# One-core transformer stack on Trainium2: router and adapter biases added by VectorE, the relative attention's output bias issued ahead of its products, and linear attention's score matmuls in alternating halves

## The chip, the cores and the metric

The kernel runs on one core of one Trainium2 chip. The metric is the device time of one launch in microseconds (us): the median over several runs. Two versions of one program are compared.

## The reference

Eight layers are applied, one after the other, to x of shape (8, 512, 128) in float32: x = x + layer(layernorm(x)). Cut to the four layers that the change touches:

```python
# ffn (twice): mixture of 8 experts, each token weighs its best 2
logits = xt @ Ws + bs
topk_w, topk_idx = top_k(logits, 2); topk_w = softmax(topk_w)
combine = sum(one_hot(topk_idx, 8) * topk_w[..., None], axis=1)
y = (silu(xt @ Wg[e]) * (xt @ Wu[e])) @ Wd[e]           # per expert e
out = einsum('ted,te->td', y, combine)
# linear attention: 16 heads of 64
weights = (queries @ keys^T / 8) * decay                  # masked scores
out = (weights @ values + beta * values) @ Wout
# adapter (twice): weights top_w of 2 adapters from the mean over all tokens
h = gelu(x @ down_w^T + down_b) * top_w
out = h @ up_w^T + (top_w[:, :, None] * up_b).sum(axis=1)[:, None, :]
# relative attention: 16 heads of 8, softmax with relative positions
out = attention(...) @ Wp.T + bp
```

The other layers are two softmax attentions without biases.

## The kernel before

One batch element of 512 tokens is one turn, and a hardware loop makes eight turns. x stays in on-chip memory through all eight layers of a turn. Tokens are cut into NT = 4 tiles of 128. Every engine runs its own program, written out by hand in the order of the layers (`pe_norm`, `pe_attn`, `pe_norm`, `pe_moe`, and so on for TensorE, with `act_...`, `pool_...` and VectorE's functions beside them). They meet at semaphores alone, so nothing but the order of the code and these waits sets what runs when.

Between two layers stands the norm. VectorE adds the layer's result to x in two halves of two tiles (`add_to_x`, L1312), takes mean and variance, GpSimd computes the inverse deviation (L437), VectorE writes the rows (L1303), TensorE transposes them (L790), and ScalarE copies them to xnT (L596). The next layer's first matmul waits for xnT.

Places that the change and the prediction touch:

- Router (`pe_moe`, L964 and L965). For each token tile one matmul of xnT with Ws (8 columns) and one of a row of ones with the bias row, both into bank 6. After the fourth pair `m_logit` lets VectorE start its chain over the logits (from L1397 on), and TensorE starts the experts' gate and up products (L984 and L988, 512 columns). VectorE's first product for the experts (L1441) is queued behind the chain over the logits. The third up product waits for it.
- Linear attention (`pe_lin`). For each of eight pairs of heads c, `scores(c)` makes two times four matmuls (L1047), head 2c on partitions 0 to 63 into bank 0, head 2c+1 on partitions 64 to 127 into bank 1. VectorE masks each bank (L1496). `states(c)` (L1059) follows, ScalarE copies its result (L695), VectorE sums it (L1504, L1505), and `outputs(c)` (L1074, L1078), one iteration later, waits for that sum. From c = 3 on `transposes(c-3)` (L1087) closes the iteration, and ScalarE copies it (L685) ahead of the next copy of states.
- Adapter (`pe_adapter`). Four down products (L1109), a small gate product, a transpose of the mixing weights (L1115, ScalarE copies it in L712), then per token tile four up matmuls (L1122) and one matmul of the mixing weights with `up_b` (L1123), 8 rows deep, into the same bank. The first up matmul waits for L712's copy, for the gelus (L710) and for VectorE's scaled up weights (L1559).
- Output projection of the attentions (`pe_out`). Four transposes (L839), ScalarE's copy (L761 in relative attention), then per tile one matmul (L844), in relative attention followed by one of a row of ones with the bias row (L846), which lies on partition 96.

A float32 matmul of this kernel stands in the trace as two records with a weight load (PEld) each; a transpose is one record.

Of the kernel before, what the change touches and what calls it, by code (L numbers as in the profile page):

```python
# [74 lines left out]
def build(nc, a_x, a_wq, a_wk, a_wv, a_wo, b_wattn, b_wout, m_ws, m_bs, m_wg, m_wu, m_wd,  # L75
# [10 lines left out]
    with ExitStack() as ctx:  # L86
# [3 lines left out]
        def sem(name):  # L90
            return ctx.enter_context(nc.semaphore(name))
# [29 lines left out]
        bs_row = wd[96:97, 2, NF - 1, 0:E]  # L121
# [119 lines left out]
        def bank(n):  # L241
# [117 lines left out]
        d_wTs = sem("ad_mix_column")  # L359
        d_y = sem("ad_up_products")  # L360
# [14 lines left out]
            (ws[:, :], m_ws), (bs_row, m_bs.rearrange("(a n) -> a n", a=1)),  # L375
# [328 lines left out]
        def act_adapter(eng, n):  # L704
# [7 lines left out]
            eng.activation(d_wT[0:E, :], bank(5)[0:E, 0:P], ACT.Copy).then_inc(d_wTs, 1)  # L712
# [123 lines left out]
        def pe_out(eng, n, w_out, bias):  # L836
# [3 lines left out]
            m.then_inc(a_oT, 1)  # L840
            eng.wait_ge(a_oTs, n + 1)
            for t in range(NT):
                o = bank(1 + t // 2)[:, P * (t % 2):P * (t % 2) + P]
                m = eng.matmul(o, xnT[:, P * t:P * t + P], w_out, start=True, stop=bias is None)  # L844
                if bias is not None:
                    m = eng.matmul(o, ones_row, bias, start=False, stop=True)  # L846
                if t % 2 == 1:
                    m.then_inc(a_y, 1)
# [111 lines left out]
        def pe_moe(eng, n):  # L960
            eng.wait_ge(experts_in, 16 * len(expert_loads))
            eng.wait_ge(xnT_ok, 2 * n + 2)
            for t in range(NT):
                eng.matmul(bank(6)[:, E * t:E * t + E], xnT[:, P * t:P * t + P], ws[:, :], start=True, stop=False)  # L964
                m = eng.matmul(bank(6)[:, E * t:E * t + E], ones_row, bs_row, start=False, stop=True)  # L965
# [28 lines left out]
        def pe_lin(eng):  # L994
# [44 lines left out]
            def scores(c):  # L1039
                for r in range(2):  # L1040
                    h = 2 * c + r
                    if h >= 2:
                        eng.wait_ge(l_wts, h - 1)
                    else:
                        eng.wait_ge(l_qk, 2 * NC2)
                    for t in range(NT):
                        m = eng.matmul(bank(r)[:, P * t:P * t + P], l_kT[64 * r:64 * r + 64, c, P * t:P * t + P],  # L1047
                                       l_qT[64 * r:64 * r + 64, c, P * t:P * t + P], start=True, stop=True)
                    m.then_inc(l_sc, 1)
# [56 lines left out]
        def pe_adapter(eng, n):  # L1106
# [8 lines left out]
            eng.transpose(bank(5)[0:E, 0:P], d_w[:, :], ident[:, :]).then_inc(d_wTp, 1)  # L1115
            eng.wait_ge(d_wTs, n + 1)
            eng.wait_ge(d_hs, KD * (n + 1))
            eng.wait_ge(d_ups, n + 1)
            for t in range(NT):
                o = bank(4 + t // 2)[:, P * (t % 2):P * (t % 2) + P]  # L1120
                for k in range(KD):
                    eng.matmul(o, d_hid[:, k, P * t:P * t + P], d_up[:, k, :], start=(k == 0), stop=False)  # L1122
                m = eng.matmul(o, d_wT[0:E, :], up_b[:, :], start=False, stop=True)  # L1123
                if t % 2 == 1:
                    m.then_inc(d_y, 1)

# [582 lines left out]
```

## Time and profile before

| | |
|---|---|
| median of 3 runs | 4981.29 us (4979.67 to 5001.24) |
| profiled execution | 4969.21 us, its span 4967.5 us |
| busy: TensorE, VectorE, ScalarE, GpSimd | 90%, 48%, 35%, 17% of the span |
| mean granted TensorE clock | 0.912 of full speed |
| chain that ended last | TensorE 80% |
| DMA over the span | 17.25 MB, 3 GB/s |

The share of busy time counts matmuls by modelled ends; the clock is one of two levels, 1.0 (2.4 GHz) or 0.5 (1.2 GHz), and 0.912 is its mean. Times below are microseconds from the start of the span, in the profiled execution.

### The profile page before, as it was taken

How to read it: one execution, taken by the hardware profiler on the slowest of the kernel's cores; microseconds unless marked ns; L12 is line 12 of the kernel's file. 1: busy time of each engine (PE TensorE's matmuls, PEld its weight loads, DVE VectorE, ACT ScalarE, POOL GpSimd, SP SyncE). 2: the span in 40 equal slices, each digit the busy share in tenths (PEclk: the TensorE clock that was granted, in tenths of full speed). 3: DMA queues.
4: the chain of work that ended last, by engine and by line, in shares of the span. 5: the costliest groups of instructions: out<-in, count | busy, mean ns of one | idle time of the engine just before them, and what ended most of it. 6: DMA issues, size and time to landing. Idle time of an engine off the chain costs nothing.

```text
span 4967.5 us, 76834 instructions
## 1 busy us (share of the span) xinstructions
PE 4473.0 (90%) x30219; PEld 2776.4 (56%) x30275; DVE 2379.6 (48%) x6906; ACT 1719.1 (35%) x3496; POOL 843.7 (17%) x1441
## 2 busy tenths in 40 slices
PE   7998989889898898988989889899898998989989
PEld 3556645565455654556545575455754457545575
DVE  3435634356443554435544355444554445544455
ACT  2322432325333343333433234333343333433334
POOL 2003110031100311103011040111401114011130
PEclk8989979999899998999989999899998999998989
DMA  2000000000000000000000000000000000000000
GB/s 68 1 1 1 1 6 1 1 1 1 6 1 1 1 1 6 1 1 1 1 6 1 1 1 1 6 1 1 2 1 6 1 1 2 1 3 1 1 1 3
DMA packets 19571, 17.25 MB, mean 3 GB/s; under 512 B 2462, under 2 KB 18799, under 8 KB 19183
## 3 DMA queue, kind: packets, MB, share of 16 engines
q1 hardware_dynamic: 19183, 11.99, 0.8%
q8 instruction: 254, 4.16, 0.4%
q14 instruction: 134, 1.10, 0.1%
HBM read 9.89 MB, written 2.10 MB: 2 GB/s over the span
## 4 chain that ended last, share of the span: by engine, by line
PE 80%; DVE 6%; POOL 6%; ACT 5%; issue 3%; DVEq 0%; ACTq 0%; POOLq 0%; SPq 0%
PE banks L984 7%; PE banks L974 7%; PE banks L988 7%; PE banks L880 7%; PE banks L908 6%; PE banks L825 6%; PE banks L920 3%; POOL work L478 3%; PE banks L865 3%; PE banks L1180 3%; PE banks L1201 2%; PE banks L1167 2%; PE banks L1074 2%; PE banks L1047 2%; PE banks L1023 2%
## 5 line engine op out<-in xcount | busy, mean ns | idle before, releaser
L1369 DVE CUSTOM_DVE_ANT_0 work<-banks,mask_row 128x512 f32<-128x512 f32 (+3 forms) x1024 | 451.6, 488 | 274.0 <-PE banks L880 270.6
L880 PE MATMUL banks<-work 32*128 32x512 f32 (+3 forms) x2048 | 526.7, 493 | 11.4 <-DVE work L1369 11.4
L908 PE MATMUL banks<-work 32*128 32x256 f32 (+3 forms) x2048 | 512.7, 504 | 20.8 <-ACT work L638 20.8
L638 ACT ACTIVATE work<-banks 128x384 f32<-128x384 f32 (+1 forms) x768 | 368.9, 526 | 441.9 <-PE banks L908 440.3
L437 POOL TENSOR_TENSOR rstd<-rstd,half 128x2 f32<-128x2 f32 x128 | 87.5, 703 | 2451.2 <-DVE moments L1297 1834.2
L654 ACT ACTIVATE work<-banks 128x512 f32<-128x512 f32 (+1 forms) x384 | 228.8, 596 | 687.6 <-PE banks L984 687.4
L1441 DVE TENSOR_TENSOR work<-work,banks 128x512 f32<-128x512 f32 (+1 forms) x384 | 263.5, 686 | 344.8 <-PE banks L988 344.5
L984 PE MATMUL banks<-xnT,wg 128*128 128x512 f32 (+1 forms) x768 | 417.8, 627 | 0.0
L988 PE MATMUL banks<-xnT,wu 128*128 128x512 f32 (+1 forms) x768 | 406.1, 611 | 0.0
L447 POOL TENSOR_SCALAR_AFFINE_SELECT work<-work 128x128 f32<-128x128 f32 (+1 forms) x768 | 252.6, 332 | 897.4 <-ACT work L638 886.1
L974 PEld LDWEIGHTS banks<-wd,work 128*128 128x128 f32 (+1 forms) x3072 | 360.6, 191 | 57.3 <-issue 57.3
L880 PEld LDWEIGHTS banks<-work 32*128 32x128 f32 x2048 | 259.0, 198 | 216.8 <-DVE work L1369 141.3
L974 PE MATMUL banks<-wd,work 128*128 128x128 f32 (+1 forms) x3072 | 361.0, 274 | 0.0
L1599 DVE TENSOR_TENSOR work<-work,banks 128x512 f32<-128x512 f32 (+1 forms) x384 | 229.2, 599 | 269.6 <-PE banks L1169 238.1
L908 PEld LDWEIGHTS banks<-work 32*128 32x128 f32 x2048 | 252.3, 198 | 125.3 <-ACT work L638 80.0
L825 PE MATMUL banks<-work,values 128*9 128x512 f32 (+3 forms) x1024 | 290.7, 433 | 0.0
L790 PE MATMUL banks<-ident,xn 128*128 128x128 f32 x256 | 85.3, 418 | 215.2 <-DVE xn L1303 212.4
L749 ACT ACTIVATE work<-banks 128x512 f32<-128x512 f32 x256 | 139.1, 595 | 377.3 <-PE banks L1201 377.3
L1426 DVE SCALAR_TENSOR_TENSOR x<-banks,work,x 128x128 f32<-128x128 f32 x512 | 144.2, 344 | 248.3 <-PE banks L974 248.3
L988 PEld LDWEIGHTS banks<-xnT,wu 128*128 128x128 f32 (+1 forms) x768 | 143.8, 187 | 206.1 <-issue 206.1
L740 ACT ACTIVATE work<-banks,work 128x512 f32<-128x512 f32 (+3 forms) x512 | 229.5, 543 | 43.4 <-DVE work L1604 43.4
L1604 DVE TENSOR_REDUCE work<-banks 128x1 f32<-128x512 f32 (+3 forms) x512 | 216.4, 483 | 22.9 <-PE banks L1180 22.9
(255 smaller groups left out, 7254.4 us busy)
## 6 DMA issues: line engine op xcount, KB each, us to landing
x_next<-in_L_attn_a_x_dram SPq DMA_DIRECT2D x8, 256.0 KB, 2.8
out_dram<-x SPq DMA_DIRECT2D x8, 256.0 KB, 2.2
wg<-in_L_ffn_Wg_dram SPq DMA_DIRECT2D x1, 1376.0 KB
wu<-in_L_ffn_Wu_dram SPq DMA_DIRECT2D x1, 1376.0 KB
wd<-in_L_ffn_Wd_dram SPq DMA_DIRECT2D x2, 512.0 KB
wk_l<-in_L_attn_a_Wk_dram SPq DMA_DIRECT2D x1, 512.0 KB, 7.8
wv_l<-in_L_attn_a_Wv_dram SPq DMA_DIRECT2D x1, 512.0 KB, 6.5
wq_l<-in_L_attn_a_Wq_dram SPq DMA_DIRECT2D x1, 512.0 KB, 7.2
```

Of the source, the lines that this page charges most:

```text
L447: eng.affine_select(out=v, in_=v, compare_op=ALU.is_ge, fill=0.0, base=0, pattern=[[0, 2], [1, P]] if j == 2 else [[1, P]], channel_multip ...
L638: eng.activation(prob4[:, G % 2, hh, C_AT[j]:C_AT[j] + C_N[j]], bank(3 + c % 3)[:, 0:C_N[j]], ACT.Exp).then_inc(s_exp, 1)
L740: eng.activation(r_prob[:, h % 2, at[t]:at[t] + (t + 1) * P], bank(bk)[:, col:col + (t + 1) * P], ACT.Exp, bias=r_neg_max[:, h % 2, t:t + ...
L825: m = eng.matmul(bank(bk)[row:row + HD + 1, P * s:T], values[:, s, h, :], p_cols[:, h % 2, at:at + T - P * s], start=(s == 0), stop=(s == ...
L880: m = eng.matmul(bank(k % 3)[:, col:col + N], q4[own, G, P * t:P * t + P], k4[own, G, 0:N], start=True, stop=True)
L908: m = eng.matmul(bank(3 + c % 3)[:, col:col + N], k4[own, G, P * s:P * s + P], q4[own, G, P * s:T], start=True, stop=True)
L974: m = eng.matmul(bank(4 + e % 2)[:, P * t:P * t + P], hidden[0:w, e % 2, j, P * t:P * t + P], wd[0:w, e, j, :], start=(j == 0), stop=(j == ...
L984: eng.matmul(bank(i % 2)[0:w, :], wg[:, e, f0:f0 + w], xnT[:, :], start=True, stop=True).then_inc(m_g, 1)
L988: eng.matmul(bank(2 + i % 2)[0:w, :], wu[:, e, f0:f0 + w], xnT[:, :], start=True, stop=True).then_inc(m_u, 1)
L1369: m = eng.tensor_tensor_reduce(out=summed[:, k % 2, col:col + N], in0=bank(k % 3)[:, col:col + N], in1=mask_row[:, T - N:T], scale=1.0, sc ...
L1441: eng.tensor_tensor(hidden[0:w, e % 2, j, :], silu[0:w, i % 2, :], bank(2 + i % 2)[0:w, :], ALU.mult).then_inc(m_h, 1)
L1599: eng.tensor_tensor(v, v, bank(k % 2)[:, 0:JOB_N[j]], ALU.add).then_inc(r_sum, 1)
```

## The change

Four things are edited.

1. Router: the four bias matmuls go. The bias is loaded once, spread over all partitions (`bs_all`), and VectorE's copy of the logits becomes an addition of it.
2. Adapter: of the four bias matmuls one stays, issued after the first tile's up matmuls, into bank 7. VectorE adds that bank to all four tiles of x in one operation ahead of `add_to_x`, which waits for it. The transposed mixing weights go to bank 6, and TensorE waits for ScalarE's copy of them only ahead of the bias matmul.
3. Relative attention's projection: the four bias matmuls are issued ahead of the wait for ScalarE's copy, and the products add to them.
4. Linear attention: `scores(c)` loops over tiles outside and halves inside, with one wait for both halves' earlier masks at its start.

```diff
@@ loads
-        bs_row = wd[96:97, 2, NF - 1, 0:E]
+        bs_all = sb("bs_all", [P, E])
-            (ws[:, :], m_ws), (bs_row, m_bs.rearrange("(a n) -> a n", a=1)),
+            (ws[:, :], m_ws), (bs_all[:, :], bass.AP(m_bs.tensor, m_bs.offset, [[0, P], [1, E]])),
@@ act_adapter
-            eng.activation(d_wT[0:E, :], bank(5)[0:E, 0:P], ACT.Copy).then_inc(d_wTs, 1)
+            eng.activation(d_wT[0:E, :], bank(6)[0:E, 0:P], ACT.Copy).then_inc(d_wTs, 1)
@@ pe_out
             m.then_inc(a_oT, 1)
+            out = [bank(1 + t // 2)[:, P * (t % 2):P * (t % 2) + P] for t in range(NT)]
+            if bias is not None:
+                for t in range(NT):
+                    eng.matmul(out[t], ones_row, bias, start=(t % 2 == 0), stop=False, skip_group_check=True)
             eng.wait_ge(a_oTs, n + 1)
             for t in range(NT):
-                o = bank(1 + t // 2)[:, P * (t % 2):P * (t % 2) + P]
-                m = eng.matmul(o, xnT[:, P * t:P * t + P], w_out, start=True, stop=bias is None)
-                if bias is not None:
-                    m = eng.matmul(o, ones_row, bias, start=False, stop=True)
+                m = eng.matmul(out[t], xnT[:, P * t:P * t + P], w_out, start=bias is None, stop=True,
+                               skip_group_check=True)
@@ pe_moe
-                eng.matmul(bank(6)[:, E * t:E * t + E], xnT[:, P * t:P * t + P], ws[:, :], start=True, stop=False)
-                m = eng.matmul(bank(6)[:, E * t:E * t + E], ones_row, bs_row, start=False, stop=True)
+                m = eng.matmul(bank(6)[:, E * t:E * t + E], xnT[:, P * t:P * t + P], ws[:, :], start=True, stop=True)
@@ pe_lin, scores(c)
-                for r in range(2):
-                    h = 2 * c + r
-                    if h >= 2:
-                        eng.wait_ge(l_wts, h - 1)
-                    else:
-                        eng.wait_ge(l_qk, 2 * NC2)
-                    for t in range(NT):
+                if c >= 1:
+                    eng.wait_ge(l_wts, 2 * c)
+                else:
+                    eng.wait_ge(l_qk, 2 * NC2)
+                for t in range(NT):
+                    for r in range(2):
                         m = eng.matmul(bank(r)[:, P * t:P * t + P], l_kT[64 * r:64 * r + 64, c, P * t:P * t + P],
                                        l_qT[64 * r:64 * r + 64, c, P * t:P * t + P], start=True, stop=True)
-                    m.then_inc(l_sc, 1)
+                        if t == NT - 1:
+                            m.then_inc(l_sc, 1)
@@ pe_adapter
-            eng.transpose(bank(5)[0:E, 0:P], d_w[:, :], ident[:, :]).then_inc(d_wTp, 1)
-            eng.wait_ge(d_wTs, n + 1)
+            eng.transpose(bank(6)[0:E, 0:P], d_w[:, :], ident[:, :]).then_inc(d_wTp, 1)
             eng.wait_ge(d_hs, KD * (n + 1))
             eng.wait_ge(d_ups, n + 1)
             for t in range(NT):
                 o = bank(4 + t // 2)[:, P * (t % 2):P * (t % 2) + P]
                 for k in range(KD):
-                    eng.matmul(o, d_hid[:, k, P * t:P * t + P], d_up[:, k, :], start=(k == 0), stop=False)
-                m = eng.matmul(o, d_wT[0:E, :], up_b[:, :], start=False, stop=True)
+                    m = eng.matmul(o, d_hid[:, k, P * t:P * t + P], d_up[:, k, :], start=(k == 0), stop=(k == KD - 1))
                 if t % 2 == 1:
                     m.then_inc(d_y, 1)
+                if t == 0:
+                    eng.wait_ge(d_wTs, n + 1)
+                    eng.matmul(bank(7)[:, 0:P], d_wT[0:E, :], up_b[:, :], start=True, stop=True).then_inc(d_bias, 1)
@@ VectorE, moe
-                link(eng.tensor_copy(lg[:, :, :], bank(6)[:, 0:NT * E].rearrange("p (t e) -> p t e", t=NT)))
+                link(eng.tensor_tensor(lg[:, :, :], bank(6)[:, 0:NT * E].rearrange("p (t e) -> p t e", t=NT),
+                                       bs_all[:, :].unsqueeze(1).to_broadcast([P, NT, E]), ALU.add))
@@ VectorE, adapter
                 i.then_inc(d_ups, 1)
+                eng.wait_ge(d_bias, n + 1)
+                eng.tensor_tensor(x[:, :, :], x[:, :, :], bank(7)[:, 0:P].unsqueeze(1).to_broadcast([P, NT, P]),
+                                  ALU.add).then_inc(d_based, 1)
+                eng.wait_ge(d_based, n + 1)
                 return add_to_x(4, d_y, n)
```

TensorE's instructions at the adapter, a row for each run of equal ones (output, operands, shape, how many). Before:

```order
L1109 MATMUL banks<-xnT,downT 128x512 x3
L1115 MATMUL banks<-ident,work 8x128
L1122 MATMUL banks<-work 128x128 x4
L1123 MATMUL banks<-up_b,work 128x128
L1122 MATMUL banks<-work 128x128 x4
L1123 MATMUL banks<-up_b,work 128x128
L1122 MATMUL banks<-work 128x128 x4
L1123 MATMUL banks<-up_b,work 128x128
L1122 MATMUL banks<-work 128x128 x4
L1123 MATMUL banks<-up_b,work 128x128
L790 MATMUL banks<-ident,xn 128x128 x4
```

In the changed kernel (L1124 are the up matmuls, L1129 is the bias, with what they wait for):

```order
L1118 MATMUL banks<-ident,work 8x128 [waits ad_mix]
L1124 MATMUL banks<-work 128x128 [waits ad_up_scaled,ad_hidden]
L1124 MATMUL banks<-work 128x128 x3
L1129 MATMUL banks<-up_b,work 128x128 [waits ad_mix_column]
L1124 MATMUL banks<-work 128x128 x12
```

Three bias matmuls have gone, and the wait for the mixing column has moved behind the first four up matmuls.

TensorE's instructions at the end of relative attention, before (w_r is the output weight, wd the tile in which the ones and the bias row lie):

```order
L839 MATMUL banks<-ident,xn 128x128 x4
L844 MATMUL banks<-w_r,xnT 128x128
L846 MATMUL banks<-wd 128x128
L844 MATMUL banks<-w_r,xnT 128x128
L846 MATMUL banks<-wd 128x128
L844 MATMUL banks<-w_r,xnT 128x128
L846 MATMUL banks<-wd 128x128
L844 MATMUL banks<-w_r,xnT 128x128
L846 MATMUL banks<-wd 128x128
```

And in the changed kernel:

```order
L841 MATMUL banks<-ident,xn 128x128 x4
L846 MATMUL banks<-wd 128x128 x4
L849 MATMUL banks<-w_r,xnT 128x128 x4
```

The four bias matmuls stand together behind the transposes, and the four products stand together behind them.

VectorE's instructions at the end of the adapter in the changed kernel (L1567 is the new addition, L1316 `add_to_x`):

```order
L1564 TENSOR_SCALAR work<-upT,work 128x128 x3
L1567 TENSOR_TENSOR x<-x,banks 128x512 [waits ad_mixed_bias]
L1316 TENSOR_TENSOR x<-x,banks 128x256 [waits ad_up_products,ad_bias_added]
L1299 BN_STATS stats<-x 128x6 [waits layer_done]
L1299 BN_STATS stats<-x 128x6
```

One operation over all of x has come in between the scaling of the up weights and the first half's addition.

## Rows read from the trace of the kernel before

**Rows 1.** The page, part 4: the chain that ended last, by engine.

```profile
PE 80%; DVE 6%; POOL 6%; ACT 5%; issue 3%; DVEq 0%; ACTq 0%; POOLq 0%; SPq 0%
```

**Rows 2.** Groups of instructions by line: records | busy us, mean ns | idle before.

```profile
L965 PE MATMUL banks<-wd 1*128 1x8 f32 x128 | 37.9, 367 | 0.0
L1123 PE MATMUL banks<-up_b,work 8*128 8x128 f32 x128 | 30.9, 321 | 0.0
```

**Rows 3.** Timeline of TensorE at a router: start, length, engine, line, records.

```profile
899.34 0.57 PE L964 MATMUL banks<-ws,xnT 128*128 128x8 f32 x2 [0.56 <-ACT xnT L596]
899.84 0.59 PE L965 MATMUL banks<-wd 1*128 1x8 f32 x2
...
903.50 1.22 PE L984 MATMUL banks<-xnT,wg 128*128 128x512 f32 x1
```

**Rows 4.** Timeline of TensorE at linear attention's beta logits.

```profile
974.52 1.86 PE L998 MATMUL banks<-wbeta,xnT 128*128 128x16 f32 x8 [0.56 <-ACT xnT L596]
976.22 1.20 PE L1023 MATMUL banks<-xnT,wq_l 128*128 128x512 f32 x1
```

**Rows 5.** Windows: busy per engine; behind POOL's the granted clock, DMA share, GB/s.

```profile
899.30:903.50 4.20, 4.16 (x16) 4.00 (x17) 0.00 (x0) 0.00 (x0) 0.00 (x0) 0.50 0.02 4
903.50:908.50 5.00, 5.00 (x7) 2.18 (x7) 4.04 (x13) 2.11 (x3) 0.00 (x0) 0.50 0.00 0
974.50:976.20 1.70, 1.68 (x8) 1.70 (x9) 0.00 (x0) 1.18 (x1) 0.67 (x1) 0.50 0.00 0
976.20:980.20 4.00, 4.00 (x8) 1.75 (x8) 0.75 (x2) 1.63 (x4) 0.00 (x0) 0.50 0.00 0
```

**Rows 6.** Timeline behind another router (first L984 at 748.64).

```profile
752.36 0.68 DVE L1441 TENSOR_TENSOR work<-work,banks 128x512 f32<-128x512 f32 x1
...
754.03 0.16 PEld L988 LDWEIGHTS banks<-xnT,wu 128*88 128x88 f32 x1 [0.27 <-issue]
```

**Rows 7.** Timeline of an adapter, up matmuls and bias matmuls.

```profile
641.15 0.25 ACT L712 ACTIVATE work<-banks 8x128 f32<-8x128 f32 x1
641.45 1.16 PE L1122 MATMUL banks<-work 128*128 128x128 f32 x8 [0.82 <-ACT work L712]
...
642.95 1.16 PE L1122 MATMUL banks<-work 128*128 128x128 f32 x8
...
647.04 0.48 PE L1123 MATMUL banks<-up_b,work 8*128 8x128 f32 x2
```

**Rows 8.** Timeline at the end of relative attention.

```profile
1861.33 0.66 PE L839 MATMUL banks<-ident,xn 128*128 128x128 f32 x4 [0.68 <-DVE xn L1348]
...
1862.67 0.49 PE L844 MATMUL banks<-w_r,xnT 128*128 128x128 f32 x2 [0.69 <-ACT xnT L761]
...
1866.50 0.79 PE L846 MATMUL banks<-wd 1*128 1x128 f32 x2
```

**Rows 9.** Timeline of linear attention's output products.

```profile
1067.45 7.41 PE L1101 MATMUL banks<-wout_l,work 128*128 128x128 f32 x64 [0.69 <-ACT work L685]
```

**Rows 10.** Timeline: the scores of c = 2.

```profile
1025.38 1.71 PE L1047 MATMUL banks<-work 64*128 64x128 f32 x16
```

**Rows 11.** Windows, L1047 alone: matmuls (x) and weight loads (x) in flight in 0.01 us.

```profile
1025.86:1025.87 0.01, 0.01 (x3) 0.01 (x2) 1.00 0.00 0
1026.20:1026.21 0.01, 0.01 (x4) 0.01 (x4) 1.00 0.00 0
```

**Rows 12.** Timeline: linear attention's first masks, sum and outputs.

```profile
1019.13 1.29 DVE L1496 TENSOR_TENSOR work<-banks,keep_ge 128x512 f32<-128x512 f32 x2 [0.49 <-PE banks L1047]
...
1022.42 0.29 DVE L1505 TENSOR_TENSOR work<-work 128x128 f32<-128x128 f32 x1
...
1022.78 0.52 PEld L1074 LDWEIGHTS banks<-work 128*128 128x128 f32 x4
```

**Rows 13.** Timeline: linear attention's last two iterations.

```profile
1051.80 0.60 ACT L685 ACTIVATE work<-banks 128x512 f32<-128x512 f32 x1 [4.21 <-PE banks L1087]
...
1054.00 0.53 PEld L1074 LDWEIGHTS banks<-work 128*128 128x128 f32 x4
...
1057.15 0.60 ACT L685 ACTIVATE work<-banks 128x512 f32<-128x512 f32 x1 [4.21 <-PE banks L1087]
...
1059.02 0.93 PEld L1074 LDWEIGHTS banks<-work 128*128 128x128 f32 x4 [2.14 <-issue]
```

More of the change, by code:

```diff
@@ L359, in build @@
         d_wTs = sem("ad_mix_column")
+        d_bias = sem("ad_mixed_bias")
+        d_based = sem("ad_bias_added")
         d_y = sem("ad_up_products")
```

## The prediction

> **What bounds the kernel now.** I read the page's chain first: TensorE holds 80% of it, so time taken from TensorE's own stream counts unless a wait appears in its place [rows 1]. The groups by line give the size of the bias matmuls: 128 records of 37.9 us at the routers and 128 of 30.9 us at the adapters, none with idle time ahead of it [rows 2]. Busy time does not say what a removal is worth, so each place was read in the timeline: router, adapter, projection, scores. The windows give the clock that was granted there.
>
> **Router (edit 1).** A router's stretch runs from 899.34 to the first gate product at 903.50: 4.16 us for 16 records, one per 0.26 us [rows 3]. The nearest thing without bias matmuls is linear attention's beta product: four matmuls of the same weights' size, 8 records, 974.52 to the next product at 976.22, 1.70 us [rows 4]. Both run at the slow clock, 0.50 [rows 5]. So a router loses 4.16 - 1.70 = 2.46 us, and two routers in each of eight turns lose 16 x 2.46 = 39 us. The lower bound is that the products behind give half of it back through the clock (rival A), the upper one that they give none and the clock rises earlier. VectorE's addition in place of a copy is an operation on 32 columns; even at the price of a 512-column one, 0.68 us, it is covered: the chain over the logits ends in front of the L1441 at 752.36, that product is done at 753.04, and the weight load that waits for it starts only at 754.03, 1.0 us later [rows 6]. Were that cover gone, it would cost up to 0.68 us a router, 11 us. The broadcast load of 32 bytes per partition is issued once, at the start, and I count it as nothing.
>
> **Adapter (edit 2).** One record of this shape follows the other every (7.41 - 0.27) / 63 = 0.113 us where nothing interrupts them [rows 9]. A tile with its bias takes 642.95 - 641.45 = 1.50 us, of which eight up records need 8 x 0.113 = 0.90; the bias costs 0.60, far above its two records, since TensorE pauses ahead of it and behind it [rows 7]. Before, the stretch is 641.45 to 647.52, 6.07 us. After, the first tile with its bias takes 1.50, the second starts anew with 1.16 for eight records, and two more take 16 x 0.113 = 1.81: 4.47 us, a gain of 1.60. The start moves too: it waited for L712's copy, which began at 641.15 [rows 7], and now waits for the gelu that ends shortly behind that. The bounds are 0 and 0.30, I take 0.15. Together 1.75 us, 16 times: 28 us. VectorE's new operation covers 512 columns from a bank, as L1441 does in 0.68 us [rows 6]. The bias is ready some 1.5 us into the stretch, so it ends near 2.3 us, and the second tile's matmuls, for which `add_to_x` waits, end near 2.7 us. It is hidden behind them, with 0.4 us to spare; without that cover it would still be hidden ahead of the second half, because VectorE's first half and statistics have 1.8 us of matmuls over them. What is queued behind it on VectorE is the first half's addition alone.
>
> **Relative projection (edit 3).** In the typical turn products and biases run from 1862.67 to 1867.29, 4.62 us; TensorE had been free since 1861.99 [rows 8]. A matmul's two records last 0.79 us there when the clock has fallen, 0.49 before. After, the four biases start near 1862.0 and take what eight records of that size take, 1.16 us less the end of the last, and one pause of 0.2: the products start near 1863.0, 0.35 us later than before. They then run on for 1.16 us [as rows 7], to 1864.2. That is 3.1 us less. If the clock is fast throughout before too, each change between product and bias costs half of the adapter's (0.60 - 2 x 0.113), 0.19 us [rows 7, 9], a step of two records 0.42 us, eight of them 3.4 us, and the gain is 1.9; if it is slow throughout, everything about doubles and the gain is 2.4. I take 2.7 us, eight times: 22 us, between 15 and 25.
>
> **Scores in alternating halves (edit 4).** Sixteen records in sequence would need 16 x 0.113 + 0.16 = 1.97 us [rows 9]. They take 1.71 [rows 10], and in the middle of the stretch four matmuls and four weight loads are in flight where there were three and two before [rows 11]: the second half already runs beside the end of the first. If the halves run beside each other all the way, they take what eight records take, 1.16 us, 0.55 less. Not all of it arrives. In c = 0 and 1 VectorE sets the pace: both masks end at 1020.42 and the next scores need both; the outputs start at 1022.78, right behind the sum that ends at 1022.71 [rows 12]. Neither moves. From c = 4 on a chain takes over: transposes, ScalarE's copies L685 and L695, VectorE's sum, then the outputs. In the last iteration, where no scores cover it, it takes 1059.02 - 1057.15 = 1.87 us; one iteration earlier the outputs start 1054.00 - 1051.80 = 2.20 us behind the same copy [rows 13]. So 0.33 of the 0.55 us is worth something there. A turn gains 2 x 0.55 (c = 2, 3) + 4 x 0.33 = 2.4 us, eight turns 19 us. The bounds are 0 (the hardware orders them no better) and 8 x 8 x 0.55 = 35 us.
>
> **Sum.** 39 + 28 + 22 + 19 = 108 us. The profiled execution took 4969.2 us, which gives 4861; the median of the runs lies 12 us above that execution, and I put it back on: 4873 us.
>
> **Rivals.**
>
> A. The clock takes back half of the router's gain. The matmuls with 8 columns run at the slow clock, and so do the first products behind them, 4 to 5 us of them [rows 5]. If the clock rises at a set distance from the start of the router, 2.46 us of 512-column products move into the slow stretch and cost twice their time: 16 x 1.23 = 20 us less gain, 4893 us. Against it: the products are slow for 5.0 us behind a start of 4.16 us and for 4.0 us behind one of 1.70 us, so the rise follows the wide products more than the first matmul [rows 3 to 5].
>
> The Trainium skill, "TensorE: Matmul & The Clock Gate", Part 1, says that the warm-up is a budget of time and not a number of matmuls, and that whatever is issued in it runs at half speed. By that rule rival A's 4893 us would be the result. The trace leaves it open, since the slow stretch behind a short start is not longer by what the start is shorter.
>
> B. Alternation gives nothing, because VectorE's masks or the copies hold the loop. For it: one chain already stands within 0.33 us of deciding [rows 13]. Then 4892 us.
>
> C. The adapter's new addition comes late and holds the norm. That needs the 0.4 us of slack gone; it costs at most 0.68 us, 16 times: 4884 us.
>
> D, slower. Every change of half costs TensorE what the adapter's bias costs in its place, 0.60 us per matmul of two records [rows 7]. Eight matmuls take 4.8 us instead of 1.71, 3.1 us more for each of 64 pairs of heads, 198 us; with the other edits' 89 us gained the kernel comes out at 5090. The point from which it decides is (1.71 + 89/64) / 8 = 0.39 us for a matmul. Against it: halves do overlap where they meet [rows 11], and the bias shares its rows of the array with the matmuls around it, which the halves do not.
>
> **How the numbers follow.** The forecast, all four edits near their sizes, gets 0.66; A 0.13, B 0.12, C 0.04, D 0.05. The range goes down to 4845 (the alternation's upper bound and a clock that falls less often, as TensorE's stretches of small matmuls get shorter) and up to 4908, which holds A, B and C, and most of A with B (4912). What a measurement can tell from no change is about 0.5%, 25 us. All cases but D are faster than that, save a remainder.
>
> **What would show it.** Router: first router record to first gate product 1.7 us, where it was 4.16. Adapter: first up matmul to the last 4.5 us, with VectorE's new operation over before the second tile's matmuls. Projection: first product later by 0.3 us, last one ending 1.2 us behind it. Scores: 16 records in 1.2 us, periods of 5.0 us where they were 5.35 in the later iterations, and new idle time of TensorE ahead of L1074's counterpart. A: the slow stretches behind the routers longer by 2 us. D: scores above 3 us. The forecast is wrong if the clock is granted less in the experts' products, if an iteration of linear attention stays at 5.35 us, or if another stage, which no edit touches, waits more.

## The result, and the profile after

The changed kernel takes 4823.22 us, median of 4 runs (4816.55 to 4831.63), beside 4980.48 us for the kernel before on the same chip. The ratio is 0.9681, 95% interval 0.9645 to 0.9716: 157 us faster. The forecast was 4873 us, its range 4845 to 4908, so the kernel ends 50 us below the forecast and 22 us below the range. Medians take every run; ratios leave out runs that lie over 1.5% above the fastest of the same program. The profiled execution took 4821.89 us, span 4820.2 us, mean granted clock 0.929; before it was 4969.21, 4967.5 and 0.912.

The page of the changed kernel: busy time, the clock in 40 slices, and the chain that ended last.

```profile
PE 4323.8 (90%) x30051; PEld 2656.8 (55%) x30051; DVE 2385.6 (49%) x6922; ACT 1718.7 (36%) x3496; POOL 841.7 (17%) x1441
...
PEclk8999999999899999999989999999998999999989
...
PE 79%; DVE 7%; POOL 7%; ACT 4%; issue 3%; DVEq 0%; POOLq 0%; ACTq 0%; SPq 0%
```

The page of the kernel before, the clock line.

```profile
PEclk8989979999899998999989999899998999998989
```

The chain is what it was, to within a percentage point in each engine [rows 1]. The clock line is not: a 7 is gone and there are fewer 8s. Both programs are now read at the four places of the forecast.

**Router.** The changed kernel's timeline, TensorE and the addition of the bias.

```profile
866.62 1.85 PE L968 MATMUL banks<-ws,xnT 128*128 128x8 f32 x8 [0.56 <-ACT xnT L598]
868.32 1.20 PE L987 MATMUL banks<-xnT,wg 128*128 128x512 f32 x1
...
868.50 0.19 DVE L1401 TENSOR_TENSOR work<-banks,bs_all 128x32 f32<-128x32 f32 x1 [2.98 <-PE banks L968]
```

From the first record to the first gate product it is 1.70 us, where it was 4.16 [rows 3], to the hundredth what was forecast. The addition in place of the copy is 0.19 us long.

**Adapter.** The changed kernel's timeline.

```profile
624.04 0.69 ACT L712 ACTIVATE work<-banks,down_b 128x512 f32<-128x512 f32 x1 [0.17 <-PE banks L1112]
624.63 0.25 ACT L714 ACTIVATE work<-banks 8x128 f32<-8x128 f32 x1
...
624.78 1.16 PE L1124 MATMUL banks<-work 128*128 128x128 f32 x8 [0.67 <-ACT work L712]
...
625.87 0.48 PE L1129 MATMUL banks<-up_b,work 8*128 8x128 f32 x2
...
626.29 2.95 PE L1124 MATMUL banks<-work 128*128 128x128 f32 x24
626.39 0.69 DVE L1567 TENSOR_TENSOR x<-x,banks 128x512 f32<-128x512 f32 x1 [2.70 <-PE banks L1129]
627.55 0.42 DVE L1316 TENSOR_TENSOR x<-x,banks 128x256 f32<-128x256 f32 x1 [0.47 <-PE banks L1124]
```

The up products now wait for the gelu (L712) and start 0.15 us behind the start of the copy of the mixing column (L714), where it was 0.30 [rows 7]. They end at 629.24, 4.46 us behind their start (forecast 4.47, before 6.07). VectorE's new operation ends at 627.08, and the addition behind it begins 0.47 us later, released by TensorE and not by it.

**Relative attention's projection.** The changed kernel's timeline.

```profile
1807.88 0.65 PE L841 MATMUL banks<-ident,xn 128*128 128x128 f32 x4 [0.68 <-DVE xn L1352]
...
1808.46 1.15 PE L846 MATMUL banks<-wd 1*128 1x128 f32 x8
1808.57 0.60 ACT L763 ACTIVATE xnT<-banks 128x512 f32<-128x512 f32 x1 [2.08 <-PE banks L841]
...
1809.54 1.16 PE L849 MATMUL banks<-w_r,xnT 128*128 128x128 f32 x8
```

From the first transpose to the end of the products it is 1810.70 - 1807.88 = 2.82 us, before 1867.29 - 1861.33 = 5.96 [rows 8]. The biases fill the time of ScalarE's copy, and eight product records stand in one row of 1.16 us. All eight turns show this at the fast clock.

**Scores in alternating halves.** The changed kernel's timeline in two late iterations of linear attention.

```profile
1606.89 1.16 PE L1049 MATMUL banks<-work 64*128 64x128 f32 x16
1606.99 0.60 ACT L687 ACTIVATE work<-banks 128x512 f32<-128x512 f32 x1 [3.88 <-PE banks L1090]
...
1608.49 0.29 DVE L1510 TENSOR_TENSOR work<-work 128x128 f32<-128x128 f32 x1
...
1608.86 0.52 PEld L1077 LDWEIGHTS banks<-work 128*128 128x128 f32 x4
...
1611.90 1.16 PE L1049 MATMUL banks<-work 64*128 64x128 f32 x16
```

Sixteen records take what eight take, 1.16 us, where they took 1.71 [rows 10]. The period is 1611.90 - 1606.89 = 5.01 us, before 5.35. The outputs start right behind VectorE's sum (1608.86 beside 1608.78), so the chain from the copy to the sum does decide there, as read from [rows 13].

So all four places came out as forecast, and the kernel is still 50 us faster than forecast.

**Where the rest is.** I cut each turn into its stages, from the first transpose of one norm (L790, in the changed kernel L792) to that of the next. Means over the eight turns of the profiled executions, in us; the last column is the time that TensorE spends at the slow clock, 0.5. The eighth turn's last adapter ends the program, so the column of the second adapter is a mean over seven.

| | attention 1 | experts 1 | attention 2 | experts 2 | linear | adapter 1 | relative | adapter 2 | turn | slow clock |
|---|---|---|---|---|---|---|---|---|---|---|
| before | 81.92 | 74.86 | 80.09 | 75.04 | 105.01 | 17.09 | 161.05 | 22.50 | 617.56 | 109.2 |
| after | 80.16 | 72.38 | 79.49 | 72.39 | 100.75 | 15.87 | 157.35 | 20.81 | 599.19 | 85.5 |

Eight turns give 8 x 18.37 = 147 us. Experts 41 (forecast 39), linear attention 34 (19), adapters 23 (28), relative attention 30 (22), and the two softmax attentions, where nothing was edited, 19 (0). That is 39 us more than the 108 of my sum. The other 11 are the 12 us by which I set the median above the profiled execution: the changed kernel's median stands 1 us above its own.

### The profile page after: what moved, and what is told of

Read it like the earlier page. It is cut to its first block, busy times and chain, and to the rows that moved or that the text cites. A ratio compares the mean times of both kernels' runs of the same rounds, so it can differ in the third digit from the quotient of the medians.

```text
span 4820.2 us, 76474 instructions
## 1 busy us (share of the span) xinstructions
PE 4323.8 (90%) x30051; PEld 2656.8 (55%) x30051; DVE 2385.6 (49%) x6922; ACT 1718.7 (36%) x3496; POOL 841.7 (17%) x1441
## 3 DMA queue, kind: packets, MB, share of 16 engines
q8 instruction: 254, 4.16, 0.4%
## 4 chain that ended last, share of the span: by engine, by line
PE 79%; DVE 7%; POOL 7%; ACT 4%; issue 3%; DVEq 0%; POOLq 0%; ACTq 0%; SPq 0%
PE banks L987 7%; PE banks L991 7%; PE banks L977 7%; PE banks L884 7%; PE banks L827 6%; PE banks L912 6%; POOL work L480 4%; PE banks L924 3%; PE banks L869 3%; PE banks L1184 3%; PE banks L1205 3%; PE banks L1171 2%; PE banks L1077 2%; PE banks L1112 2%; PE banks L1026 2%
## 5 line engine op out<-in xcount | busy, mean ns | idle before, releaser
L792 PE MATMUL banks<-ident,xn 128*128 128x128 f32 x256 | 85.3, 411 | 220.6 <-DVE xn L1307 217.7
```

## The experiments

Theory after the result: each edit gives its local time, and the rest comes from TensorE's clock, which is granted at 0.5 in other stretches when the stages shift by a few us. Rival: the edits interact, one of them unlocks time in a stage that it doesn't touch. Second rival: a single edit holds the surplus.

**One edit alone.** Four kernels, each with one of the four parts of the diff above and nothing else. The router alone:

```diff
-                eng.matmul(bank(6)[:, E * t:E * t + E], xnT[:, P * t:P * t + P], ws[:, :], start=True, stop=False)
-                m = eng.matmul(bank(6)[:, E * t:E * t + E], ones_row, bs_row, start=False, stop=True)
+                m = eng.matmul(bank(6)[:, E * t:E * t + E], xnT[:, P * t:P * t + P], ws[:, :], start=True, stop=True)
...
-                link(eng.tensor_copy(lg[:, :, :], bank(6)[:, 0:NT * E].rearrange("p (t e) -> p t e", t=NT)))
+                link(eng.tensor_tensor(lg[:, :, :], bank(6)[:, 0:NT * E].rearrange("p (t e) -> p t e", t=NT),
+                                       bs_all[:, :].unsqueeze(1).to_broadcast([P, NT, E]), ALU.add))
```

> The kernel before with the router's edit alone. If an edit is worth its own stretch, both router stages lose 2.5 us a turn each and the rest stays: 39 us less, ratio 0.992. If the surplus over the forecast comes from the clock that the other stages are granted, the stages that this edit does not touch change too, by up to some 3 us a turn either way, and the total lands anywhere between 15 and 65 us less; the sum of the slow-clock time then explains the difference from 39 us at half its size.

Median of its six runs 4966.94 us beside 4971.66, 5 us less; the ratio, 0.9842 (0.9779 to 0.9905), is that of the three fastest. By the medians neither reading in the expectation came true, 39 us or 15 to 65. These six are the most telling of the study: one program, and its runs are

| us | 4861.3 | 4864.4 | 4927.3 | 5006.6 | 5013.6 | 5018.2 |
|---|---|---|---|---|---|---|
| granted clock | 0.939 | 0.937 | 0.917 | 0.894 | 0.892 | 0.890 |

They span 157 us, as much as the whole change gives. The time at the slow clock is 2 x (1 - clock) x time: 593 us in the fastest, 1104 in the slowest, so a microsecond at the slow clock costs 157 / 511 = 0.31 us. The three fastest alone give nearly the same, 66 us of time for 225 us at the slow clock, 0.29.

Adapter alone (the two parts on the adapter):

```diff
-                m = eng.matmul(o, d_wT[0:E, :], up_b[:, :], start=False, stop=True)
...
+                if t == 0:
+                    eng.wait_ge(d_wTs, n + 1)
+                    eng.matmul(bank(7)[:, 0:P], d_wT[0:E, :], up_b[:, :], start=True, stop=True).then_inc(d_bias, 1)
```

> The kernel before with the adapter's edit alone. Own stretch: 1.6 us less per adapter in the up matmuls and 0 to 0.3 at their start, 26 to 28 us in all, ratio 0.9945. Clock theory: the untouched stages move by as much again, either way.

4987.03 us (4949.62 to 5009.48), ratio 1.0036 (1.0016 to 1.0056).

Relative projection alone (`pe_out`):

```diff
+            if bias is not None:
+                for t in range(NT):
+                    eng.matmul(out[t], ones_row, bias, start=(t % 2 == 0), stop=False, skip_group_check=True)
             eng.wait_ge(a_oTs, n + 1)
```

> The kernel before with the relative projection's edit alone. Own stretch: the products end 2.0 to 3.4 us earlier per turn, 22 us in all (15 to 27), ratio 0.9955. Clock theory: also the norm and the adapter behind it, and the next turn, are granted another clock.

4998.84 us, ratio 1.0056 (1.0031 to 1.0081).

Scores alone (`scores(c)`):

```diff
-                for r in range(2):
+                for t in range(NT):
+                    for r in range(2):
                         m = eng.matmul(bank(r)[:, P * t:P * t + P], l_kT[64 * r:64 * r + 64, c, P * t:P * t + P],
                                        l_qT[64 * r:64 * r + 64, c, P * t:P * t + P], start=True, stop=True)
```

> The kernel before with the alternating halves alone. Own stretch: 0.55 us less in c = 2 and 3 and 0.33 us in c = 4 to 7, 2.4 us a turn, 19 us in all, ratio 0.996; the scores take 1.16 us in every iteration. Clock theory: the stage of linear attention changes by more than 2.4 us where its outputs or its end fall into another clock, and the stages without an edit move too. If the four edits alone add up to about 157 us, the effects are local; if they add up to 108 us or to something unrelated, what is left comes from the place of the stages against the clock.

4983.23 us, ratio 1.0019 (1.0005 to 1.0034).

Three of the four are no faster than before, where 26 to 28, 22 and 19 us less were expected. Stage means again, each from one profiled execution. These are not all typical: that of the router (4864 us) and that of the adapter (4950) are among the fastest of their runs, that of the projection (5017) is the slowest of eight. So they are read stage by stage and not for the total.

| | attention 1 | experts 1 | attention 2 | experts 2 | linear | adapter 1 | relative | turn | slow clock |
|---|---|---|---|---|---|---|---|---|---|
| router | 78.54 | 72.05 | 78.13 | 72.06 | 103.73 | 16.72 | 161.34 | 604.50 | 76.7 |
| adapter | 79.56 | 75.25 | 83.14 | 74.99 | 106.42 | 15.52 | 159.48 | 615.11 | 109.9 |
| projection | 84.94 | 75.26 | 84.91 | 74.54 | 104.85 | 17.64 | 159.11 | 623.63 | 130.7 |
| scores | 79.26 | 75.25 | 83.14 | 74.99 | 105.56 | 17.64 | 161.32 | 619.00 | 119.8 |

The experts lose 2.8 us with the router's edit and nothing without it; adapter 1 is 1.6 us shorter with the adapter's. The scores' edit alone leaves the linear stage no shorter, 105.56 us beside 105.01, because 23.4 us of it are at the slow clock, where it was 14.5; its scores take 1.16 us in every iteration, as expected, and its late periods 5.01. With the projection's edit the relative stage is 1.9 us shorter, while both softmax attentions are 3 and 5 us longer than before, and nothing in them was edited. The windows show what differs there. Columns: stretch, its length, then busy time of PE, PEld, DVE, ACT and POOL, and the granted clock. Before, first and second attention of a turn:

```profile
1278.00:1358.60 80.60, 72.65 (x504) 37.77 (x504) 37.07 (x160) 31.43 (x63) 17.10 (x51) 0.88 0.01 2
1433.60:1511.90 78.30, 69.87 (x505) 35.23 (x505) 37.01 (x160) 32.33 (x64) 17.14 (x51) 0.96 0.00 1
```

The changed kernel, first attention in two turns:

```profile
1233.10:1314.00 80.90, 72.89 (x505) 38.17 (x505) 37.52 (x160) 31.56 (x63) 17.11 (x51) 0.88 0.01 2
1834.30:1912.60 78.30, 69.89 (x505) 35.33 (x505) 37.05 (x160) 31.03 (x63) 17.13 (x51) 0.95 0.01 3
```

Scores alone, second attention of one turn and first of a later one:

```profile
1418.30:1506.20 87.90, 80.48 (x505) 40.79 (x505) 37.40 (x160) 32.96 (x64) 17.08 (x51) 0.80 0.00 1
1886.60:1964.90 78.30, 69.92 (x504) 35.25 (x504) 36.92 (x160) 31.03 (x63) 16.99 (x51) 0.95 0.01 3
```

The same instructions, VectorE and ScalarE about as busy as ever, and 78.3, 80.6 to 80.9 or 87.9 us, in the order of the clock: 0.95 or 0.96, 0.88, 0.80. It happens between two attentions of one execution as between two programs.

**The same program, shifted.** If place against the clock is what matters, a pause that touches no stage must move the kernel as much as an edit does. At the end of each turn, when all of x is done, VectorE copies x into a tile that nobody reads then, k times. Kernel before and changed kernel, k = 2 and 6:

```diff
+                eng.wait_ge(x_done, 16)
+                for _ in range(k):
+                    link(eng.tensor_copy(xn[:, :, :], x[:, :, :]))
                 eng.nop().then_inc(ended, 1)
```

> The kernel before with two additional copies of x (128x512, VectorE alone, nothing reads them) at the end of every turn, some 1 us more per turn, nothing else. If the length of a stage does not depend on when it begins, the kernel is 8 us slower and every stage keeps its length. Clock theory: attention stages without any edit take another of the lengths 78, 81, 85 or 88 us, and the kernel moves by anything between 60 us less and 60 us more.

> The same with six additional copies, some 3 us more per turn: 24 us slower without the clock; by the clock theory again anything between 40 us less and 80 us more, and not in proportion to the run with two copies.

> The changed kernel with two additional copies per turn. Without the clock: 8 us above the changed kernel. Clock theory: the surplus of 49 us over the sum of the edits is luck of the start times, so most delays give part of it back, up to 60 us slower than the changed kernel.

> The changed kernel with six additional copies per turn. Without the clock: 24 us above the changed kernel. Clock theory: between 30 us less and 80 us more. Over several delays the mean gap between changed kernel and kernel before at the same delay should come near 108 us if the edits are worth what their own stretches show, and stay near 157 us if the surplus belongs to the edits.

The timeline of the kernel before with two copies has them as one row.

```profile
647.73 0.89 DVE L1682 COPY xn<-x 128x512 f32<-128x512 f32 x2
```

To place these four I ran k = 1 and 4 too, with the same edit.

> The kernel before with one additional copy of x per turn (0.45 us by the run with two). Clock theory: the attention stages, which nothing edits, take 78, 81, 85 or 88 us, and the total lies anywhere from 4950 to 5080 us. Additive theory: 4 us slower than before.

> The kernel before with four additional copies per turn, 1.8 us. Clock theory: 4950 to 5080 us. Additive theory: 14 us slower than before.

> The changed kernel with one additional copy per turn. Clock theory: 4790 to 4950 us. With the delays 0, 1, 2, 4 and 6 the mean over the alignments of the changed kernel lies 108 us under that of the kernel before if the edits are worth their own stretches, more if they also make the clock fall less often whatever the alignment.

> The changed kernel with four additional copies per turn. Clock theory: 4790 to 4950 us, and between the runs with two copies (4799) and six (4948) only by chance. Additive theory: 14 us slower than the changed kernel, 4838 us.

Medians, and ratio to the kernel before in the same comparison (the changed kernel without copies is that of the result, above):

| copies, their time a turn | kernel before | changed kernel |
|---|---|---|
| 0 | 4976.24 | 4823.22, 0.9681 (0.9645 to 0.9716) |
| 1, 0.45 us | 4969.46, 0.9983 (0.9969 to 0.9998) | 4818.11, 0.9673 (0.965 to 0.9696) |
| 2, 0.89 us | 5032.16, 1.0075 (1.005 to 1.01) | 4798.99, 0.9617 (0.9592 to 0.9642) |
| 4, 1.8 us | 5022.85, 1.0088 (1.0067 to 1.0109) | 4828.25, 0.9684 (0.965 to 0.9719) |
| 6, 2.7 us | 4998.02, 1.0035 (1.0016 to 1.0054) | 4947.60, 0.9922 (0.9893 to 0.9952) |

Two copies are 7 us of added work over eight turns. They cost the kernel before 51 us by the medians (4980.67 in that comparison), 37 by the ratio, and give the changed one 24. Six are 22 us of work and cost the changed kernel 124. Its softmax attentions are the place; here, with six copies:

```profile
1251.40:1339.60 88.20, 80.81 (x504) 40.98 (x504) 37.41 (x160) 31.68 (x63) 17.07 (x51) 0.79 0.01 2
1412.50:1500.30 87.80, 80.39 (x504) 40.70 (x504) 37.46 (x160) 32.96 (x64) 17.06 (x51) 0.80 0.00 1
```

The page of the changed kernel with six copies, the clock line, and below it that with two.

```profile
PEclk9999979899798997889978999789997899978999
```

```profile
PEclk8989999999999999999999999999999998999989
```

The means over the five shifts are 5000 us before and 4843 after, again 157 us apart. Single values lie up to 105 us from their mean, so this mean gap is sure to some 30 us only (its standard error). The expectation above was: near 108 us if the edits are worth their own stretches, near 157 if the surplus belongs to them too. It came out at 157, but 108 lies only 1.7 standard errors away, so five shifts do not decide it. By stage the mean turn is 19.85 us shorter: 17.75 in stages that were edited (142 us over eight turns), 2.1 in the two that weren't (17 us). The edited stages are shorter in this mean by 5.2 us (experts), 5.4 (linear), 3.1 (adapters) and 4.1 (relative).

**One edit left out.** The changed kernel with one part put back, diffs as above with the signs turned.

> The changed kernel without the router's edit. Own stretches: 39 us slower than the changed kernel (4862 us). If the surplus hangs on this edit, it is 80 us slower or more (4900 us); by the clock alone anything from 4790 to 4970.

> The changed kernel without the adapter's edit. Own stretches: 28 us slower than the changed kernel (4851 us); if the surplus hangs on it, 75 us or more.

> The changed kernel without the relative projection's edit. Own stretches: 22 us slower than the changed kernel (4845 us); if the surplus hangs on it, 70 us or more.

> The changed kernel without the alternating halves. Own stretches: 19 us slower than the changed kernel (4842 us); if the surplus hangs on it, 65 us or more.

| left out | us | ratio to before | costs | turn | slow clock a turn |
|---|---|---|---|---|---|
| router | 4945.07 | 0.9939 (0.9916 to 0.9962) | 122 | 616.71 | 125.3 |
| adapter | 4934.47 | 0.9919 (0.9894 to 0.9945) | 111 | 612.96 | 117.0 |
| projection | 4855.87 | 0.9769 (0.9732 to 0.9806) | 33 | 602.01 | 94.3 |
| scores | 4855.01 | 0.9663 (0.9619 to 0.9708) | 32 | 603.33 | 87.5 |

"Costs" is the median less 4823.22 us, which is of another comparison; by the ratios the four cost 128, 118, 44 and -9 us. So what the scores' edit is worth in the set can't be read from totals: its ratio is that of the runs of 4807, 4807 (clock 0.947) and 4855 us (0.928), and two more took 4910 and 4915. The expectations of router and adapter named 80 and 75 us or more as the sign that the surplus hangs on that edit, and both came above it. The adapter's edit costs 111 us when it is taken out of the set, and gains nothing when it is put in alone, where its own two stages are 3.3 us a turn shorter, 26 us. Without it the slow clock takes 117.0 us a turn instead of 85.5. Most of that time lies in the softmax attentions: 82.6 and 86.1 us without the router's edit, 84.9 and 83.5 without the adapter's, 80.2 and 79.5 with all four. So no single edit holds the surplus, since leaving out either of two loses it. The rival that edits unlock each other would need a wait or a stage that two of them share; the attentions share none with them, their instructions and waits are unchanged, and a pause of 2.7 us brings the same lengths with all four edits in place.

A straight line through the turns of the 18 profiled executions (the four edits as yes or no, the number of copies, the slow time; means of the first seven turns) leaves 0.95 us a turn unexplained; without the slow time it leaves 4.75. Its slope is 0.33 us for each at the slow clock, beside 0.31 from the six runs above. At equal slow time it gives the edits 3.6, 3.2, 0.8 and 2.9 us a turn (router, adapter, projection, scores; each to 0.6 to 0.9). The bias matmuls of the router, and the end of relative attention that the projection's edit shortens, were themselves at the slow clock in the kernel before, for 4.9 and 5.5 us a turn; at 0.33 that is 3.4 us more. Together 14.0 us a turn, 112 in eight (to some 6), beside 108 in the forecast: what the edits do themselves was forecast well.

**Can the clock be kept up?** The changed kernel and that with six copies, with 12 matmuls more in each softmax attention. They are not part of the computation: their results go to a bank that nobody reads.

```diff
+                if k in (8, 12, 16, 20):
+                    if k == 8:
+                        eng.wait_ge(a_v, n + 1)
+                    for _ in range(3):
+                        eng.matmul(bank(7), q4[own, G, 0:P], k4[own, G, :], start=True, stop=True)
```

> The changed kernel with twelve additional matmuls of 32 rows and 512 columns in each softmax attention, among the row scores, where TensorE waits for VectorE's row maxima. They compute nothing that is read. If the clock falls there because the array is thinly used, the falls some 21 us into these stages disappear, and the stages take 78 us in every turn: up to 28 us less than the changed kernel. If they only take TensorE's time, the stages take 1 to 3 us more each.

> The same additional matmuls in the changed kernel with six additional copies per turn, whose attention stages take 88 us. If the fill keeps the clock up, they fall to 78 to 81 us and the kernel from 4948 to about 4840 us; if not, it stays at 4948 or above.

5187.19 us (ratio 1.0431, 1.0391 to 1.047) and 5187.31 (1.0435, 1.0397 to 1.0473). The attentions grew to 101 and 102 us in the mean. Windows of the first of them, both attentions of a turn:

```profile
1321.60:1422.60 101.00, 92.45 (x529) 46.04 (x529) 37.64 (x160) 31.48 (x63) 17.08 (x51) 0.79 0.01 2
1495.40:1597.00 101.60, 93.42 (x529) 46.75 (x529) 37.70 (x160) 32.76 (x64) 17.13 (x51) 0.77 0.00 1
```

More matmuls in the thin stretch did not keep the clock up: these stages have 44 and 48 us at the slow clock, where they had 15 and 13. They have 32 rows like those around them. Nor did they cost the 1 to 3 us that I expected otherwise, but 20 to 23: the twelve are 24 records in a stage, and one lasts 0.94 us. What does keep the clock up is open. The place where it falls can be seen in the kernel before; TensorE's timeline and the windows around it:

```profile
1297.88 2.79 PE L880 MATMUL banks<-work 32*128 32x256 f32 x10 [0.71 <-DVE work L1369]
...
1301.22 1.65 PE L880 MATMUL banks<-work 32*128 32x512 f32 x3
```

```profile
1296.00:1298.00 2.00, 1.29 (x17) 0.86 (x14) 0.81 (x5) 0.69 (x1) 0.00 (x0) 1.00 0.00 0
1298.00:1300.00 2.00, 2.00 (x9) 1.32 (x10) 1.83 (x13) 0.00 (x0) 0.00 (x0) 1.00 0.00 0
1300.00:1302.00 2.00, 2.00 (x9) 0.92 (x8) 2.00 (x7) 0.00 (x0) 0.00 (x0) 0.77 0.00 0
1302.00:1304.00 2.00, 2.00 (x10) 0.83 (x6) 0.85 (x4) 0.00 (x0) 0.00 (x0) 0.50 0.00 0
```

TensorE waits 0.71 us for VectorE, then works on 32 of its 128 rows; between 1300 and 1302 us the clock goes from 1.00 to 0.50, while the engine counts as wholly busy. In the second attention of the same turn, 78.3 us long, the same instructions run without such a fall: its 7 us at the slow clock all lie in the first 7.5 us of the stage. So this stretch alone does not make the clock fall.

## Why the prediction was off, point by point

- **Router.** Right: 4.16 to 1.70 us, 41 us against 39. Rival A was wrong. The slow stretch of the products behind a router is 3.7 to 3.8 and 5.0 to 5.1 us in alternate turns, where it was 2.9 to 6.0 with a mean of 4.6; no 2 us were added to it. It had begun before the router's first record in all 32 routers of the two traces, by 1.1 to 8.3 us: it does not begin with the router. The Trainium skill's rule of a warm-up budget ("TensorE: Matmul & The Clock Gate", Part 1), by which what is issued during it runs slow, would, counted from the router, have taken half of the 2.46 us back. The trace does not agree with that reading: the experts' stages are 2.5 and 2.6 us shorter.
- **Adapter.** The stretch is 4.46 us and starts 0.15 us sooner behind the copy, both as forecast, and it holds in all sixteen (4.45 beside 6.08). The stages give 23 us in this pair and 3.1 x 8 = 25 in the mean over shifts, against 28. In this pair the difference lies ahead of the first adapter's stretch: that part is 9.06 us where it was 8.65, with 6.8 us at the slow clock where it had 3.8. Rival C was wrong: the addition was over 0.47 us before the half behind it could start, near the 0.4 I gave it.
- **Projection.** I had 2.7 us. From the first transpose to the end of the products it is 3.2 in the mean over turns (6.03 to 2.83), 26 us in eight, since the clock stays fast in all eight turns and no pauses are left. Of the rest of the stage, 1.0 us a turn comes from the part ahead of it, where nothing was edited and the slow time fell by 2.6 us, and 0.46 is lost behind it: the next norm's transposes, which wait for VectorE, start 2.83 us behind the products, where it was 2.37. I had no term for that wait. The stage gave 30 us. That the clock stays fast here is not sure either: with this edit alone the same part took 2.83 us in five turns and 4.45, with 3.6 at the slow clock, in three.
- **Scores.** Right in size and place: 0.55 us each in c = 2 and 3, 0.34 of it worth something from c = 4 on. Rivals B and D were wrong. One reading was off: the second iteration, which I took not to move, is 0.37 us shorter (4.93 to 4.56). The first and the last scores of a turn, before and in the changed kernel:

```profile
1017.94 1.71 PE L1047 MATMUL banks<-work 64*128 64x128 f32 x16
...
1051.69 1.71 PE L1047 MATMUL banks<-work 64*128 64x128 f32 x16
```

```profile
1585.60 1.16 PE L1049 MATMUL banks<-work 64*128 64x128 f32 x16
...
1616.91 1.16 PE L1049 MATMUL banks<-work 64*128 64x128 f32 x16
```

That is 33.75 and 31.31 us, 2.4 less. Up to the output products, in turns without slow time in between, it is 47.2 us without the edit (one turn before, all eight with the router's edit alone) and 44.4 with it (five turns of the changed kernel): 2.8 us a turn, 22 us against 19. The stage gave 34; the other 12 go with slow time, of which a turn's linear attention has 10.7 us where it had 14.5.
- **Sum.** This is the step that failed. "39 + 28 + 22 + 19 = 108 us" takes every stage that no edit touches, and every edited stage outside its edit, at its old length and so at its old clock. The clock was granted at 0.5 for 871 us of the span before, and for 686 after. Of these 185 us, 39 are the router's own bias matmuls and 44 lie in the projection and right behind it, where its edit works. The rest, about 102, at 0.31 us each, are some 32 us of the 39 by which the sum fell short; this is an estimate, with the slope of other runs. Most of the remaining 7 is in the terms themselves: router, projection and scores were short by 2, 4 and 3 us, and 4 were lost behind the projection. The range did name "a clock that falls less often", but gave it no size: of the 28 us from 4873 down to 4845, 16 are the upper bound of the alternation, which leaves 12. The six runs of the router's kernel show what the clock can do, 157 us in one program.
- **The 12 us put back.** "The median of the runs lies 12 us above that execution": I took this as a constant of the kernel, and it was not one. It cost 11 us. The changed kernel's median lies 1 us above its profiled execution.

What is not settled: whether the changed kernel is at the slow clock less because of its edits or by luck. Over five shifts its turns have 93.6 us of it and those before 122.6; with six copies it has 128.7. Of the 29 us between the means some 10 are the router's and the projection's own stretches. The other 19 are 1.7 times the standard error of the gap, 11 us, so they point to the edits but do not show it. By what rule the edits would lower it no run shows.

The fastest kernel of the study by its median is the changed one with two copies, 4798.99 us, ratio 0.9617 (0.9592 to 0.9642). It is 24 us faster than the changed kernel though it does more work; its turns have 78.7 us at the slow clock beside 85.5. Nobody should build on it.

## What to carry to other kernels

Where a kernel has many stages and TensorE's granted clock falls in some of them, read the time at the slow level first, in every stage. Judge a small edit by its stages' lengths at equal clock, and by the total only as a mean over several shifts; one total, and one edit alone, said here that three edits gave nothing, though each shortened its own stretch as forecast or nearly so. A forecast from local sizes needs a term for the clock in its range, of the size that runs of one program, or of the same program with a short pause put in, differ by.

## What the runs showed of the hardware

- An unedited stage takes one of few lengths: in the 18 profiled executions with unedited attentions, 287 of the 288 attention stages take 78.0 to 78.4 us (up to 8 us at the slow clock), 80.6 to 81.0 (15 to 20), 85.1 to 85.5 (30 or 31) or 87.8 to 88.2 (35 to 37).
- Turns can lock. Turns 3 to 5 of the kernel before are 614.38 to 614.39 us each; turns 2 to 5 of the changed kernel are 597.0, 601.2, 596.8 and 601.1. So a shift of 0.9 us a turn need not average out over turns.
- Matmuls on rows 0 to 63 and on rows 64 to 127, issued in turn, run beside each other: sixteen records in 1.16 us, where a half's eight in a row leave 1.71. This came as forecast.
- A matmul of 8 rows between matmuls of 128 costs far more than its records: 0.60 us for two, once again here, between the starts of the first tile's up products and the second's (626.29 - 624.78 = 1.51 us, less 8 x 0.113).
